# Normalised tokens turned by VectorE in squares of 32 by 32, over a DRAM scratch, instead of by TensorE

## The chip, the cores and the metric

The kernel runs on one core of a Trainium2 chip. The metric is the device time of one execution in microseconds; it is 1164.3 us as a median of three runs (1164.17 to 1164.88).

## What is computed

Input is x, 16 sequences of 1024 tokens with 256 features, in fp32. Two stages, each `x = x + layernorm(f(layernorm(x)))`:

```
g = sigmoid(xn @ Wg.T + bg);  h = scan over the sequence of  h = (1-g)*h + g*xn;  f = h @ Wo.T + bo
router: expert of a token = argmax(xn @ router_w + router_b); rank within the expert < 320 or overflow
f = relu(xn @ w1[e] + b1[e]) @ w2[e] + b2[e]        for a token with a place in its expert (8 of them)
f = relu(xn @ ow1 + ob1) @ ow2 + ob2                for a token that overflowed
```

The kernel sends every token through the overflow path in the loop, and scatters its row (x1, its number and statistics) to its place in a DRAM scratch; the experts then compute the rows that have a place and overwrite their output.

## The kernel before, in words

There are 32 groups of 512 tokens (TG = 4 tiles of 128), two for each sequence; a group is written (i, u), with u its parity. Every fp32 product is made of three fp32r ones (hi*hi, hi*lo, lo*hi), so every operand is split into a hi part by ScalarE and a lo part by VectorE or GpSimd.

The loop is pipelined by groups. In one step TensorE works on the hidden layers (layer1, layer2, eight blocks j of 128 features) of group `now`, on the projection of `nxt` (project) and its transposes (transposes1), and on the transposes (transposes0) and the gate of `far`, which is two groups ahead. `prev` is the group before `now`. The four compute engines run the same steps, each in an order written out by hand; only semaphores tie them.

What belongs to the first normalisation of group far (statistics number 0): VectorE's bn_stats and bn_aggr (read_rows0, moments, in the step before), then two small operations, veps = var + eps and nmean = -mean, still on VectorE; GpSimd makes rstd by pow and nmr = nmean * rstd (deviation, L396), and writes tok = x * rstd + nmr (norm0, L403). TensorE turns tok into psT by eight 128x128 transposes (transposes0, L1330, at j == 3 of the step), ScalarE copies psT to xnT_hi (xn_hi, L644), VectorE takes the rest (xn_lo, L888), and TensorE computes the gate from these at j == 5.

Statistics 1 are those of the attention's output of nxt (ScalarE's norm1, L628, needs them), 2 those of x1 of nxt (deviation2 and norm2, L434 and L443, write tok2 on GpSimd), 3 those of the overflow's output (ScalarE's norm3, L636, for prev).

Order of the step on each engine, before:

- GpSimd (L464): deviation(3, prev), norm0(far), deviation(1, nxt), renumber, norm2(nxt), four indirect stores (dispatch) of now, hst_lo (state_lo) of far.
- VectorE (L1106): low(0, 1), choose, attended and statistics 1 of nxt, residual2(prev), low(2), place(now), low(3), xn_lo(far), residual1(nxt) to x1, statistics 2, low(4, 5), recurrence(far), low(6), read_rows0, low(7), xf_lo(nxt), moments(0), result(now), statistics 3. low(j) is the lo part of hidden block j (L1012).
- ScalarE (L690): blocks 0 and 1, norm3(prev), blocks 2 and 3, xn_hi(far), norm1(nxt), blocks 4 and 5, sigmoid(far), blocks 6 and 7, xf_hi(nxt), state_hi(far).
- SP issues the plain DMAs (L314): the output store of prev, then, after x1 of nxt, the x load three groups ahead.

layer2(now, j) waits for low(j). W1[0], the weights of the first half of the experts, isn't used in the loop.

## Time and profile before

| | before |
|---|---|
| median of three runs | 1164.3 us |
| profiled execution | 1166.17 us, its span 1163.0 us |
| TensorE matmul / weight load busy | 98% / 88% |
| VectorE / ScalarE / GpSimd busy | 85% / 64% / 59% |
| busy share of the 16 DMA engines in the loop | 0.11 |
| mean granted TensorE clock | 0.997 |

The profile is of one execution. Times in it are us from the start of the span; a line such as L1012 is the line of the kernel that issued the instruction. Start-up lasts to about 90 us, the loop with its steady steps to about 950 us, then the last groups and the eight experts follow.

### The profile page before, as it was taken

What the parts mean: (1) busy time and instruction counts of PE and PEld (TensorE: products, weight loads), DVE (VectorE), ACT (ScalarE), POOL (GpSimd) and SP (SyncE); (2) the same over time, 40 slices, a digit from 0 to 9 for tenths busy, and PEclk for the clock granted to TensorE, in tenths of its full rate; (3) what the DMA queues carried; (4) which work ended last, traced back from release to release, by engine and by line L of the source; (5) the groups of instructions that cost most, each with busy time, mean ns of one, the idle gap of its engine ahead of it and who ended that gap; (6) DMA issues with size and microseconds to landing.
All of it is one profiled execution on the core that took longest, in us unless ns stands there. A gap on an engine that the chain in (4) does not pass through costs nothing.

```text
span 1163.0 us, 24424 instructions
## 1 busy us (share of the span) xinstructions
PE 1142.6 (98%) x7549; PEld 1020.4 (88%) x7549; DVE 991.5 (85%) x2741; ACT 742.1 (64%) x1375; POOL 690.1 (59%) x792
## 2 busy tenths in 40 slices
PE   8999999999999999999999999999999999999996
PEld 4788898888988898888888888988898888899996
DVE  6888988888888988989898888888888987688885
ACT  4366666666656666666666666656666666678782
POOL 3556567675656666565657665656666664414444
PEclk9999999999999999999999999999999999999998
DMA  9121110100111111111101101111111100335430
GB/s 262 58 100 56 55 46 35 43 27 30 36 36 36 36 36 36 36 36 36 36 19 35 34 23 33 36 36 36 36 36 36 36 18 20 114 114 191 145 130 34
DMA packets 59428, 65.09 MB, mean 56 GB/s; under 512 B 7835, under 2 KB 55629, under 8 KB 59268
## 3 DMA queue, kind: packets, MB, share of 16 engines
q1 hardware_dynamic: 52228, 59.36, 15.8%
q0 software_dynamic: 7168, 5.34, 1.5%
q8 instruction: 15, 0.25, 0.1%
q14 instruction: 17, 0.14, 0.0%
HBM read 40.19 MB, written 38.76 MB: 68 GB/s over the span
## 4 chain that ended last, share of the span: by engine, by line
PE 90%; DVE 5%; POOL 2%; ACT 1%; issue 1%; DMA 0%; DVEq 0%; POOLq 0%; ACTq 0%
PE psY L1430 12%; PE psY L1433 11%; PE psY L1432 11%; PE psH L1324 11%; PE psH L1325 11%; PE psH L1326 10%; PE psA L1324 5%; PE psA L1325 5%; PE psA L1326 5%; PE psT L1380 3%; PE psT L1337 2%; DVE st L859 1%; PE psT L1393 1%; PE psT L1395 1%; PE psA L1498 1%
## 5 line engine op out<-in xcount | busy, mean ns | idle before, releaser
L621 ACT ACTIVATE hid<-psH,biasT 128x512 f32<-128x512 f32 (+1 forms) x312 | 202.9, 650 | 217.6 <-PE psH L1326 215.2
L1430 PE MATMUL psY<-W_hi,hid_hi 128*128 128x256 f32 x1168 | 336.1, 288 | 0.6 <-DVE hid_lo L1012 0.5
L1433 PE MATMUL psY<-W_hi,hid_lo 128*128 128x256 f32 x1168 | 330.3, 283 | 0.0
L1432 PE MATMUL psY<-W_lo,hid_hi 128*128 128x256 f32 x1168 | 330.2, 283 | 0.0
L399 POOL TENSOR_TENSOR rstd<-veps,mhalf 128x4 f32<-128x4 f32 (+2 forms) x103 | 141.4, 1373 | 163.2 <-DVE nmean L871 163.2
L1012 DVE TENSOR_TENSOR hid_lo<-hid,hid_hi 128x512 fp32r<-128x512 f32 (+1 forms) x308 | 200.6, 663 | 42.5 <-ACT hid_hi L626 35.8
L1324 PE MATMUL psH<-xfT_hi,W_hi 128*128 128x512 f32 (+1 forms) x624 | 235.9, 378 | 0.3 <-ACT hid L621 0.2
L1325 PE MATMUL psH<-xfT_lo,W_hi 128*128 128x512 f32 (+1 forms) x624 | 234.9, 376 | 0.0
L1326 PE MATMUL psH<-xfT_hi,W_lo 128*128 128x512 f32 (+1 forms) x624 | 232.7, 373 | 0.0
L1430 PEld LDWEIGHTS psY<-W_hi,hid_hi 128*128 128x128 f32 x1168 | 222.7, 191 | 9.9 <-DVE hid_lo L1012 1.6
L1432 PEld LDWEIGHTS psY<-W_lo,hid_hi 128*128 128x128 f32 x1168 | 223.0, 191 | 5.9
L1433 PEld LDWEIGHTS psY<-W_hi,hid_lo 128*128 128x128 f32 x1168 | 223.0, 191 | 0.0
L626 ACT ACTIVATE hid_hi<-hid 128x512 fp32r<-128x512 f32 (+1 forms) x308 | 185.2, 601 | 9.8
L421 POOL DMA_INDIRECT xbuf<-x,idx x128 | 144.8, 1131 | 38.4 <-issue 37.8
L437 POOL TENSOR_TENSOR x<-veps,mhalf 128x4 f32<-128x4 f32 x32 | 44.0, 1375 | 173.9 <-DVE nmean L871 173.9
L1326 PEld LDWEIGHTS psH<-xfT_hi,W_lo 128*128 128x128 f32 x624 | 117.2, 188 | 20.9
L1324 PEld LDWEIGHTS psH<-xfT_hi,W_hi 128*128 128x128 f32 x624 | 118.1, 189 | 18.6 <-ACT hid L621 0.8
L1325 PEld LDWEIGHTS psH<-xfT_lo,W_hi 128*128 128x128 f32 x624 | 118.1, 189 | 12.8
L452 POOL TENSOR_SCALAR tok<-x 128x256 f32<-128x256 f32 x116 | 109.0, 951 | 7.7 <-POOL x L440 7.7
L640 ACT ACTIVATE ysb<-ysb,nmr,rstd 128x256 f32<-128x256 f32 x144 | 75.1, 591 | 45.2 <-POOL nmr L401 45.1
L654 ACT ACTIVATE keep<-psA,neg_bg 128x512 f32<-128x512 f32 x64 | 44.1, 689 | 67.9 <-PE psA L1326 62.6
L461 POOL TENSOR_TENSOR hst_lo<-hst,hst_hi 128x512 fp32r<-128x512 f32 x60 | 76.9, 1316 | 3.7 <-ACT hst_hi L662 3.4
(173 smaller groups left out, 2176.8 us busy)
## 6 DMA issues: line engine op xcount, KB each, us to landing
xin<-L_attn_x SPq DMA_DIRECT2D x32, 512.0 KB, 3.4
stage<-L_ffn_w SPq DMA_DIRECT2D x16, 1024.0 KB, 5.2
out<-outt SPq DMA_DIRECT2D x31, 512.0 KB, 2.8
xbuf<-zrow SPq DMA_DIRECT2D x1, 2590.0 KB, 16.5
xin<-xbuf SPq DMA_DIRECT2D x8, 259.0 KB, 4.9
stage<-L_ffn_ow SPq DMA_DIRECT2D x2, 1024.0 KB, 8.5
xbuf<-x,idx POOLq DMA_INDIRECT x128, 2.1
b_b<-L_ffn_b SPq DMA_DIRECT2D x1, 1024.0 KB, 6.5
```

Of the source, the lines that this page charges most:

```text
L399: pool.tensor_tensor(rstd[k][:, t0:n], veps[k][:, t0:n], mhalf[:, t0:n], ALU.pow).then_inc(s_rs[k], 1)
L421: pool.indirect_dma_start(out=xbuf, out_offset=bass.IndirectOffsetOnAxis(idx[v][:, t:t + 1], 0), in_=x1[v][:, t, 0:ROW], in_offset=None, b ...
L452: last = pool.tensor_scalar(tok2[:, t, :], x1[v][:, t, 0:D], x1[v][:, t, D + 1:D + 2], x1[v][:, t, D + 2:D + 3], ALU.mult, ALU.add)
L621: act.activation(hid[j % 2][:, at:n], psH[:, j % 2, at:n], ACT.Relu, bias=bias).then_inc(s_hid, 1)
L626: act.activation(hid_of(j, 0, tail)[:, at:n], hid[j % 2][:, at:n], ACT.Copy).then_inc(s_hid_hi, 1)
L1012: dve.tensor_tensor(hid_of(j, 1, tail)[:, at:n], hid[j % 2][:, at:n], hid_of(j, 0, tail)[:, at:n].bitcast(F32), ALU.subtract).then_inc(s_h ...
L1324: pe.matmul(dst, w_hi, r_hi, start=(k == 0), stop=False)
L1325: pe.matmul(dst, w_hi, r_lo, start=False, stop=False)
L1326: return pe.matmul(dst, w_lo, r_hi, start=False, stop=(k == last_k))
L1430: pe.matmul(dst, hi, w[0][:, j, :], start=(j == 0 and (tail or t % 2 == 0)), stop=False, skip_group_check=True)
L1432: pe.matmul(dst, hi, w[1][:, j, :], start=False, stop=False, skip_group_check=True)
L1433: last = pe.matmul(dst, lo_, w[0][:, j, :], start=False, stop=(j == HC - 1), skip_group_check=True)
```

## The change

Three things are changed.

1. For the groups from (2, 0) on, TensorE's transposes0 in the step is gone. SP waits for tok, stores it (512 KB) to a DRAM scratch `turnbuf` of 512 rows of 256 numbers, waits until it has landed, and issues eight loads. Each fills 32 partitions of one half of `tok_blocks` (in the unused lo part of W1[0]): partition a*32 + x gets, for n = 0 to 15, the 32 numbers `a*32 ..` of the half's columns of row n*32 + x. VectorE then turns the 32x32 squares of both halves into psT, after low(2) and ahead of place.
2. The two small operations at the end of moments go from VectorE to GpSimd, ahead of pow, in all statistics but those of the last expert's tail.
3. On GpSimd norm0(far) comes ahead of deviation(3, prev). On SP the exchange comes ahead of the output store and the x load.

```diff
+        turnbuf = nc.dram_tensor("turnbuf", [GT, D], F32).ap()
+        tok_blocks = late[1][:, 0:TG * D].bitcast(F32).rearrange("p (c n x) -> p c n x", c=DC, x=SQ)
...
+            def exchange_blocks(g):
+
+                i, v = g
+                sp.wait_ge(s_tok, cnt(g, 1, 1))
+                sp.dma_start(turnbuf.rearrange("(t p) d -> p t d", p=P), tok[:]).then_inc(s_turnbuf[v], 16)
+                sp.wait_ge(s_turnbuf[v], landed((i - 2, v)))
+                for a in range(P // SQ):
+                    for c in range(DC):
+                        cols = slice(c * P + a * SQ, c * P + (a + 1) * SQ)
+                        sp.dma_start(tok_blocks[a * SQ:(a + 1) * SQ, c, :, :],
+                                     turnbuf[:, cols].rearrange("(n x) d -> x n d", x=SQ)).then_inc(s_blocks[v], 16)
+
+            def step(i, u, later=True):
+                prev, nxt, turn, far = grp(i, u, -1), grp(i, u, 1), grp(i, u, 2), grp(i, u, 3)
+                if later and live(turn, NG):
+                    exchange_blocks(turn)
                 if live(prev, NG):
                     store(prev)
...
             def deviation(k, g, n, extra=0, t0=0):
 
+                pool.wait_ge(s_ag[k], cnt(g, 1, 1) + extra)
+                pool.sem_inc(s_held, 1)
+                pool.tensor_scalar(veps[k][:, t0:n].unsqueeze(2), mv[k][:, t0:n, 1:2], EPS, None, ALU.add).then_inc(s_ve[k], 1)
+                pool.tensor_scalar(nmean[k][:, t0:n].unsqueeze(2), mv[k][:, t0:n, 0:1], -1.0, None, ALU.mult)
                 pool.wait_ge(s_ve[k], cnt(g, 1, 1) + extra)
...
+                if live(far, NG):
+                    norm0(far)
                 if live(prev, NG):
                     deviation(3, prev, TG, t0=sure(prev))
-                if live(far, NG):
-                    norm0(far)
...
             def moments(k, g, n, base=0, t0=0):
                 dve.wait_ge(s_st[k], cnt(g, 1, 1) + base)
+                dve.wait_ge(s_nm[k], cnt(g, 1, 0) + base)
                 dve.sem_inc(s_held_v, 1)
                 for t in range(t0, n):
                     last = dve.bn_aggr(mv[k][:, t, :], st[k][:, t, :])
                 last.then_inc(s_ag[k], 1)
-                dve.wait_ge(s_nm[k], cnt(g, 1, 0) + base)
-                dve.wait_ge(s_ag[k], cnt(g, 1, 1) + base)
-                dve.tensor_scalar(veps[k][:, t0:n].unsqueeze(2), mv[k][:, t0:n, 1:2], EPS, None, ALU.add)
-                dve.tensor_scalar(nmean[k][:, t0:n].unsqueeze(2), mv[k][:, t0:n, 0:1], -1.0, None, ALU.mult)\
-                    .then_inc(s_ve[k], 1)
...
+            def turn_blocks(g):
+                i, v = g
+                dve.wait_ge(s_blocks[v], landed((i - 2, v), DC * (P // SQ)))
+                for c in range(DC):
+                    dve.transpose(psT[:, c, :], tok_blocks[:, c, :, :]).then_inc(s_T0, 1)
...
                 low(2)
+                if ahead:
+                    turn_blocks(far)
                 if run and up:
                     place(now)
...
-                    if j == 3 and ahead:
-                        transposes0(far)
```

deviation2 gets the same two operations as deviation.

## Rows read from the trace of the kernel before

**Rows 1.** The page: busy time, share of the span and instructions of each engine.
```profile
PE 1142.6 (98%) x7549; PEld 1020.4 (88%) x7549; DVE 991.5 (85%) x2741; ACT 742.1 (64%) x1375; POOL 690.1 (59%) x792
```

**Rows 2.** Stages: window, its us, busy us (count) of each engine, clock, DMA share, GB/s.
```profile
120.00:900.00 780.00, 780.00 (x5159) 699.40 (x5158) 689.33 (x1926) 499.16 (x902) 501.13 (x576) 1.00 0.11 36
...
497.45:528.59 31.14, 31.14 (x207) 27.98 (x207) 27.08 (x76) 19.96 (x36) 21.55 (x25) 1.00 0.11 34
...
1155.00:1160.00 5.00, 0.00 (x0) 0.00 (x0) 0.54 (x1) 0.00 (x0) 2.31 (x3) 0.70 0.18 66
```

**Rows 3.** TensorE in order of time (start, us), and from the waits (total, times, longest).
```profile
508.17 1.04 PE L1337 MATMUL psT<-ident,tok 128*128 128x128 f32 x8
509.04 0.18 PE L1409 MATMUL psA<-oh,upto 128*128 128x32 bf16 x1
...
PEld psT L1337 <- POOL tok L410: 4.5, 14, 0.7
```

**Rows 4.** GpSimd in order of time: start, us, what, [idle before, releaser].
```profile
498.13 2.55 POOL L461 TENSOR_TENSOR hst_lo<-hst,hst_hi 128x512 fp32r<-128x512 f32 x2
501.17 1.42 POOL L399 TENSOR_TENSOR rstd<-veps,mhalf 128x4 f32<-128x4 f32 x1 [0.49 <-DVE nmean L871]
...
503.33 1.01 POOL L399 TENSOR_TENSOR rstd<-veps,mhalf 128x4 f32<-128x4 f32 x1
...
504.86 2.17 POOL L410 TENSOR_SCALAR tok<-xin,rstd,nmr 128x256 f32<-128x256 f32 x4 [0.24 <-POOL nmr L401]
...
516.74 1.41 POOL L437 TENSOR_TENSOR x<-veps,mhalf 128x4 f32<-128x4 f32 x1 [5.79 <-DVE nmean L871]
...
527.67 2.57 POOL L461 TENSOR_TENSOR hst_lo<-hst,hst_hi 128x512 fp32r<-128x512 f32 x2
...
560.47 2.57 POOL L461 TENSOR_TENSOR hst_lo<-hst,hst_hi 128x512 fp32r<-128x512 f32 x2
```

**Rows 5.** ScalarE (one row) and VectorE in order of time.
```profile
503.49 2.08 ACT L640 ACTIVATE ysb<-ysb,nmr,rstd 128x256 f32<-128x256 f32 x4 [0.90 <-POOL nmr L401]
...
508.21 1.23 DVE L942 TENSOR_TENSOR outt<-ysb,x 128x1024 f32<-128x1024 f32 x1
509.36 0.68 DVE L1012 TENSOR_TENSOR hid_lo<-hid,hid_hi 128x512 fp32r<-128x512 f32 x1
509.97 0.18 DVE L994 TENSOR_TENSOR rk<-psA,row 128x32 f32<-128x32 f32 x1
...
515.93 0.38 DVE L866 BATCH_NORM_AGGREGATE mv<-st 128x2 f32<-128x6 f32 x4 [0.16 <-DVE st L859]
...
527.72 2.56 DVE L870 TENSOR_SCALAR veps<-mv 128x4 f32<-128x4 f32 x1
...
548.18 0.38 DVE L866 BATCH_NORM_AGGREGATE mv<-st 128x2 f32<-128x6 f32 x4 [0.16 <-DVE st L859]
```

**Rows 6.** Groups by line and shape: count, busy us, mean ns, idle before.
```profile
L431 POOL TENSOR_SCALAR x<-x 128x4 f32<-128x4 f32 x30 | 8.0, 267 | 2.7
...
L956 DVE TENSOR_TENSOR xfT_lo<-psT,xfT_hi 128x512 fp32r<-128x512 f32 x60 | 38.6, 685 | 13.9 <-ACT xfT_hi L669 13.9
```

**Rows 7.** DMA: KB, landing us; SP's issues; packets, MB, share from 509.61 to 512.41.
```profile
xin<-L_attn_x SPq DMA_DIRECT2D x32, 512.0 KB, 3.4
out<-outt SPq DMA_DIRECT2D x31, 512.0 KB, 2.8
...
514.51 0.38 SPq L272 DMA_DIRECT2D xin<-L_attn_x  x1
...
1009.95 0.48 SPq L343 DMA_DIRECT2D xin<-xbuf  x1
...
q1 hardware_dynamic: 528, 0.52, 52.8%
```

**Rows 8.** DMA packets from 14 to 15 us: number, size, share of 16 engines.
```profile
DMA packets 427, 0.09 MB, mean 89 GB/s; under 512 B 350, under 2 KB 427, under 8 KB 427
...
q1 hardware_dynamic: 427, 0.09, 60.6%
```

More of the change, by code:

```diff
@@ L26 @@
 QUAD = P // TG
+SQ = 32
 EPS = 1e-5
@@ L210, in sandwich_kernel @@
         s_T0 = sem("s_T0")
+        s_blocks = sems("s_blocks")
+        s_turnbuf = sems("s_turnbuf")
         s_xn_hi = sem("s_xn_hi")
@@ L312, in store @@
                     .then_inc(s_st_out[v], 16)
-            def step(i, u):
-                prev, nxt, far = grp(i, u, -1), grp(i, u, 1), grp(i, u, 3)
+            def exchange_blocks(g):
[12 more added lines that the diff above has]
+                    exchange_blocks(turn)
                 if live(prev, NG):
@@ L323, in _ @@
             load((1, 0))
-            step(0, 0)
+            step(0, 0, later=False)
             sp.wait_ge(s_ow_hi, 4)
@@ L329, in _ @@
             load_w2((0, 0))
-            step(0, 1)
+            step(0, 1, later=False)
             with sp.Fori(1, NG // 2 - 2) as i:
@@ L435, in deviation2 @@
                 i, v = g
+                pool.wait_ge(s_ag[2], cnt(g, 1, 1))
+                pool.sem_inc(s_held, 1)
+                pool.tensor_scalar(veps[2][:].unsqueeze(2), mv[2][:, :, 1:2], EPS, None, ALU.add).then_inc(s_ve[2], 1)
+                pool.tensor_scalar(nmean[2][:].unsqueeze(2), mv[2][:, :, 0:1], -1.0, None, ALU.mult)
                 pool.wait_ge(s_ve[2], cnt(g, 1, 1))
```

## The prediction

> **What bounds the kernel now.** I read the page first, then the table by stage, then one step of the loop engine by engine. The page gives TensorE 98% busy and VectorE 85% [rows 1]. That is an average; the table by stage says more: from 120 to 900 us TensorE is busy 780.00 of 780 us, and one step of the loop takes 31.14 us, all of it matrix work, at a granted clock of 1.00 [rows 2]. So in the steady loop nothing but TensorE sets the time, and an edit that leaves every other engine in time is worth what it takes off TensorE. Reading one step in order of time shows how much room the others have, and that is the question here, because the change lengthens one of their paths. That path is a ring, once around per step:
>
> 1. VectorE's last bn_aggr on x1 ends (515.93 + 0.38 = 516.31) [rows 5].
> 2. GpSimd ends those statistics, writes tok2, issues four scatters and does hst_lo, until 527.67 + 2.57 = 530.24: 13.93 us [rows 4, 5]. In the step of the other parity the same stretch runs from 548.56 to 563.04: 14.48. I take 14.2.
> 3. GpSimd ends statistics 3, then 0, and writes tok (one step earlier 500.68, by the same period, to 504.86 + 2.17 = 507.03: 6.35 us) [rows 4].
> 4. TensorE turns tok (0.9 us), and ScalarE copies it, then normalises att.
> 5. VectorE does place, low(3), xn_lo, the residual to x1 and its statistics, without a gap from 509.97 to 516.31: 6.34 us [rows 5].
>
> These make 14.2 + 6.35 + 0.9 + 6.34 = 27.8 us against a step of 31.14: about 3.3 us of room. That is little: TensorE's weight loads for these transposes waited for GpSimd's tok 14 times already [rows 3].
>
> **The change part by part.** The trace's own time is 1166.2 us (span 1163.0); the median of the runs is 1164.3, 1.9 below. The sum is made against 1166.2. The scratch serves 28 groups, from (2, 0) to (15, 1), one in each step of TensorE's loop; the first two groups and the two after them keep TensorE's transposes, the experts have none.
>
> *Taken away.* Eight transposes per step: the first starts at 508.17, the next work of TensorE at 509.04 [rows 3], so 0.87 us. If all else is in time: 28 x 0.87 = 24.4 us, a step of 30.27, and 1142.
>
> *Statistics.* VectorE loses two small operations per moments, and with them a stall: at 527.72 veps took 2.56 us, beside GpSimd's hst_lo of 2.57 that had begun at 527.67 [rows 5, 4]. GpSimd gains two operations on 128x4. The nearest row is its 128x4 tensor_scalar, 267 ns [rows 6], so 0.54 us for each statistics, 2.2 us per step. In stretch 2 it starts 0.43 us sooner (at 516.31 instead of 516.74), so that net +0.1 to 0.2: 14.4. The order on GpSimd is turned: norm0(far) ahead of deviation(3). Stretch 3 loses statistics 3 thereby: pow of 0 to the end of tok takes 507.03 - 503.33 = 3.70 [rows 4], plus 0.54 is 4.24 us. Behind norm0 now stands deviation(3), for which ScalarE's norm3, VectorE's residual2 and what is queued behind it wait (a rival below). With the experts, statistics moved to GpSimd cost nothing: TensorE's work there covers them. Uncovered, 8 x 0.54 = 4 us.
>
> The Trainium skill (SBUF — State Buffer, section SBUF: two separate sides) says that VectorE's operations in a 2-port mode and GpSimd's hold a shared port pair as an exclusive lock. The row of veps beside hst_lo agrees. Were this the bound, moving the operations would gain; the step is TensorE's, so by this rule alone the sum stays.
>
> *The exchange.* It goes in place of TensorE's 0.9 us between tok and psT.
> (a) SP waits for tok and stores 512 KB: the output store, of the same size and packets, lands 2.8 us after its issue [rows 7]; with 0.1 for the wait, 2.9.
> (b) SP waits for that store to land, and then issues eight loads of 64 KB, in 128-byte pieces: 4096 packets, 256 on each of 16 engines. Nothing in the trace has this form. The store's 512 packets of 1 KB moved in 52.8% of 16 x 2.8 us, so 46 ns each, 1.5 us per engine; the x loads (same packets) land after 3.4 us [rows 7], so about 1.85 us of a load's time is fixed. Cheapest: packets so cheap that SP's issue bounds. At 0.38 to 0.48 us an issue [rows 7] the eighth goes out 3.0 us after the first; with its own packets and 1.85 that is 5.2 us. Dearest: a 128-byte packet takes as long as one of 1 KB: 256 x 0.046 = 11.8, and 1.85: 13.6 us. Between them lies the one microsecond of the trace with mostly small packets (14 to 15 us: 350 of 427 under 512 bytes): busy 60.6% of 16 us, 22.7 ns per packet; by elapsed time 37 ns [rows 8]. I take 23 ns, as the nearest row: 256 x 0.023 = 5.9, and 1.85: **7.75 us**. By elapsed time it would be 11.3.
>
> On SP the exchange stands ahead of store(prev) and load(far). The output store is needed only two steps later. The x load waits for x1, which comes later in the step. Neither is late.
>
> *The sum of the ring.* 14.4 + 4.24 + 2.9 + 7.75 + 1.38 + 6.34 = **37.0 us**. The wait for the blocks stands ahead of place, low(3), xn_lo and residual1 on VectorE, which wait with it; TensorE's layer2(3) waits for low(3), and scatters, hst_lo and the next norm0 come after. So the ring closes, and since 37.0 is more than TensorE's 30.27, the step becomes 37.0 us: +5.9 against 31.14, times 28 is 164 us. 1166.2 + 164 = **1330 us**.
>
> Bounds: stretch 2 at 13.9 + 0.2 and the exchange at 5.2 give 34.2 us a step, 1252 us; the loads at 11.3 give 40.6, 1430; at 13.6, 42.9, 1495. TensorE would wait 4 us at a time. It does so only at the end of this trace: 5 us without work, granted clock 0.70 [rows 2], so on its way to 1.2 GHz. Its stretch from low(3) to hst_hi has some 3 us of room against GpSimd's, so a short fall costs little; a long one up to 3 us a step, which is why the high end isn't lower.
>
> **Rivals.**
> *Cheap packets* (the same ring): 34.2 to 35.8 us a step, 1252 to 1296. For it: a packet of 1 KB takes 46 ns, and if time went by bytes alone, 128 bytes would take 6.
> *Dear packets*, 30 ns and more: over 39.3 us a step, over 1394. For it: the elapsed time of the small packets above.
> *The order on GpSimd decides, not the transfer.* With an exchange that costs nothing extra the path would go tok, deviation(3) (2.2 us: 501.17 to 503.33), ScalarE's norm3 (2.08), residual2 (1.23), low(2) (0.68), turn [rows 4, 5]: 14.4 + 4.24 + 2.2 + 2.1 + 1.2 + 0.7 + 1.38 + 6.34 = 32.6 us, so +1.4 per step, 1207 us. It decides if store and loads together take less than 6.2 us.
> *The other side: hidden, and TensorE stays the bound.* The step is 30.27 us, 1142 us. It needs a ring of at most 30.27, so that 6.7 us of my 37.0 are not there: store and loads in 3.9 us together, where the two fixed parts alone, 1.3 and 1.85, and the issues take 6, and statistics 3 off the path. For it: VectorE loses its stalls, and GpSimd's operations could be shorter beside an idle VectorE. Against it: both would have to give several us.
> *It doesn't do what it says*: VectorE's turn into PSUM has no fast form or the blocks come out in parts; that adds 1.4 us a step or more, inside the range.
>
> **How the numbers follow.** Ring with 6.5 to 10 us for the loads (1296 to 1394): 0.47, forecast 1330. Cheap packets: 0.24. Dear packets: 0.14. Order on GpSimd (1207): 0.08. Hidden (1142): 0.05. Within 0.2% (a ring of 31, by chance): 0.02. The range 1245 to 1430 leaves out the last three and about a third of the dear ones. Faster 0.05, same 0.02, slower 0.93; 0.2% is about what a measurement of this kernel can tell from no change.
>
> **What would show it.** Right: the steady step at 34 to 40 us; VectorE idle before the transposes, released by a DMA; TensorE idle before the layer-2 matmuls, released by hid_lo; TensorE's busy share near 85%; the chain of waits going through GpSimd and DMA. GpSimd's idle time before deviation2 and norm0 small. Wrong: a step near 30.3 with TensorE full (the packets cost far less, or the ring has slack I did not see); VectorE idle before residual2 instead (the order decides); blocks that land 5 or 12 us after the store did (the price of a packet).

## The result, and the profile after

| | before | after |
|---|---|---|
| median | 1164.46 us (1164.17 to 1164.88) | 1309.74 us (1308.39 to 1311.0) |
| ratio, 95% interval | | 1.1247 (1.1228 to 1.1267) |
| span of the profiled execution | 1163.0 us | 1306.8 us |
| mean granted TensorE clock | 0.997 | 0.968 |

The change makes the kernel 12.5% slower. The forecast was 1330 us, from 1245 to 1430.

The page of after: busy time, share of the span and instructions of each engine, then two DMA issues (KB each, median us from issue to landing); then the stage that answers to [rows 2].

```profile
PE 1179.0 (90%) x7325; PEld 1018.8 (78%) x7325; DVE 977.2 (75%) x2527; ACT 737.6 (56%) x1375; POOL 751.3 (57%) x1062
...
turnbuf<-tok SPq DMA_DIRECT2D x28, 512.0 KB, 2.8
W_lo<-turnbuf SPq DMA_DIRECT2D x224, 64.0 KB, 2.3
...
120.00:900.00 780.00, 704.09 (x4317) 606.35 (x4316) 590.00 (x1537) 428.81 (x781) 481.76 (x680) 0.96 0.23 60
```

TensorE, which had no gap in this stage before [rows 2], now has 76 us of gaps (780.00 less 704.09), and needs longer for its work: 224 matmuls fewer over the whole run, but 36.4 us more of busy time than in [rows 1]. With the 24.4 us of the transposes that are gone, its work takes some 61 us longer. By the granted clock, 0.968 on average instead of 0.997, some 38 of them are a slower clock (an estimate from the span). The rest comes with the waits: the profile models where a matmul ends (here 0.28 us after its start, while the next ones start 0.12 apart), and before a wait it counts the last one as busy up to that end.

The issues of SP in one step show the period (start, us, what):

```profile
498.30 0.36 SPq L324 DMA_DIRECT2D turnbuf<-tok  x1
501.08 4.04 SPq L329 DMA_DIRECT2D W_lo<-turnbuf  x8
...
534.52 0.36 SPq L324 DMA_DIRECT2D turnbuf<-tok  x1
```

From store to store it is 534.52 - 498.30 = **36.22 us**, where it was 31.14 [rows 2]. This is one of the longer steps. From one group's place to the next (TensorE's first matmul of it, psA<-oh,upto, once for each group) the mean of 22 steps is 35.96 us, from 35.4 to 36.7; before it was 31.17. The 4.8 us times 28 steps are 134 us. The spans differ by 143.8 us: 136.5 of it between the first and the last group's place, 1.1 ahead of it and 6.2 behind, with the experts (170.5 us instead of 164.3). So nearly all of the loss is one of the loop, about the same in each step. The chain of waits by engine, before and after, says what the time consists of, and then the chain itself in order of time, from tok to the turn:

```profile
PE 90%; DVE 5%; POOL 2%; ACT 1%; issue 1%; DMA 0%; DVEq 0%; POOLq 0%; ACTq 0%
...
POOL 27%; PE 22%; issue 15%; DVE 14%; DMA 11%; SPq 7%; ACT 3%; POOLq 1%; DVEq 0%; ACTq 0%
...
498.30 2.77 DMA turnbuf<-tok
501.08 0.32 SPq L329
501.40 0.05 issue
501.45 0.48 SPq L329
...
504.63 2.38 DMA W_lo<-turnbuf
507.02 0.06 DVE psT L923
```

The chain goes through GpSimd, the DMAs, SP and VectorE; TensorE, with 90% of this chain on the page of before, has 22% of it here. Between 501.08 and 504.63 it is SP that is followed: it hands out the eight loads, the second after 0.37 us and each further one after 0.53, and only the last one's landing is waited for. VectorE and GpSimd in order of time, with the idle time before and its releaser, close the ring (these answer to [rows 4, 5]):

```profile
507.02 1.32 DVE L923 STREAM_TRANSPOSE psT<-W_lo 128x512 f32<-128x512 f32 x2 [2.68 <-DMA W_lo<-turnbuf]
...
514.06 0.38 DVE L895 BATCH_NORM_AGGREGATE mv<-st 128x2 f32<-128x6 f32 x4 [0.18 <-DVE st L887]
...
514.63 0.46 POOL L462 TENSOR_SCALAR veps<-mv 128x4 f32<-128x4 f32 x1 [10.19 <-DVE mv L895]
515.17 0.53 POOL L463 TENSOR_SCALAR nmean<-mv 128x4 f32<-128x4 f32 x1
515.67 1.03 POOL L465 TENSOR_TENSOR x<-veps,mhalf 128x4 f32<-128x4 f32 x1
516.78 0.91 POOL L468 TENSOR_TENSOR x<-nmean,x 128x4 f32<-128x4 f32 x1
517.94 3.73 POOL L480 TENSOR_SCALAR tok<-x 128x256 f32<-128x256 f32 x4 [0.24 <-POOL x L468]
...
527.23 2.54 POOL L489 TENSOR_TENSOR hst_lo<-hst,hst_hi 128x512 fp32r<-128x512 f32 x2
529.86 0.56 POOL L420 TENSOR_SCALAR veps<-mv 128x4 f32<-128x4 f32 x1
...
532.32 2.18 POOL L434 TENSOR_SCALAR tok<-xin,rstd,nmr 128x256 f32<-128x256 f32 x4 [0.30 <-POOL nmr L425]
```

GpSimd has no gap from 514.63 to 534.50 but for short ones, then tok is stored, and the ring starts again. From 498.30 to 514.44 SP, the DMAs and VectorE have the ring; GpSimd does statistics 3 and 1 meanwhile, and then idles for 10.19 us until 514.63. TensorE's side of it, and its clock behind the gap (window, its us, busy us of its matmuls, granted clock, DMA share, GB/s):

```profile
510.16 0.58 PE L1462 MATMUL psY<-W_hi,hid_hi 128*128 128x256 f32 x1 [2.67 <-DVE hid_lo L1042]
...
507.60:511.00 3.40, 0.84 (x4) 0.86 0.05 18
511.00:515.00 4.00, 4.00 (x18) 0.69 0.27 90
```

It waits 2.67 us for low(3), which stands on VectorE behind the turn, and then works 4 us at a granted clock of 0.69, so part of this time at 1.2 GHz.

Against the steps of the prediction, each as it has it, measured in the step shown (36.22 us; the mean is 35.96):

| part of the ring | predicted | measured |
|---|---|---|
| x1's bn_aggr end to hst_lo end | 14.4 | 15.33 (514.44 to 529.77) |
| first normalisation, to the end of tok | 4.24 | 4.73 (to 534.50) |
| store | 2.9 | 2.78 |
| eight loads | 7.75 (5.2 to 13.6) | 5.94 (501.08 to 507.02) |
| turn | 1.38 | 1.23 (to 508.25, where place begins) |
| place to bn_aggr end | 6.34 | 6.19 (508.25 to 514.44) |
| sum | 37.0 | 36.2 |

### The profile page after: what moved, and what is told of

Its sections match the earlier page's. It is cut to its first block, busy times and chain, and to the rows that moved or that the text cites. A ratio compares the mean times of both kernels' runs of the same rounds, so it can differ in the third digit from the quotient of the medians.

```text
span 1306.8 us, 24281 instructions
## 1 busy us (share of the span) xinstructions
PE 1179.0 (90%) x7325; PEld 1018.8 (78%) x7325; DVE 977.2 (75%) x2527; ACT 737.6 (56%) x1375; POOL 751.3 (57%) x1062
## 4 chain that ended last, share of the span: by engine, by line
POOL 27%; PE 22%; issue 15%; DVE 14%; DMA 11%; SPq 7%; ACT 3%; POOLq 1%; DVEq 0%; ACTq 0%
SPq L329 7%; DMA turnbuf<-tok 6%; POOL hst_lo L489 5%; DMA W_lo<-turnbuf 5%; POOL xbuf L445 5%; POOL tok L434 4%; PE psY L1462 3%; POOL rstd L423 3%; DVE st L887 3%; PE psY L1465 3%; PE psY L1464 3%; PE psH L1356 2%; PE psH L1357 2%; PE psH L1358 2%; POOL tok L480 2%
## 5 line engine op out<-in xcount | busy, mean ns | idle before, releaser
L1462 PE MATMUL psY<-W_hi,hid_hi 128*128 128x256 f32 x1168 | 346.9, 297 | 77.6 <-DVE hid_lo L1042 77.6
L1465 PE MATMUL psY<-W_hi,hid_lo 128*128 128x256 f32 x1168 | 338.0, 289 | 0.0
L1464 PE MATMUL psY<-W_lo,hid_hi 128*128 128x256 f32 x1168 | 337.4, 289 | 0.0
L1464 PEld LDWEIGHTS psY<-W_lo,hid_hi 128*128 128x128 f32 x1168 | 230.0, 197 | 3.7
L1465 PEld LDWEIGHTS psY<-W_hi,hid_lo 128*128 128x128 f32 x1168 | 230.6, 197 | 0.0
L462 POOL TENSOR_SCALAR veps<-mv 128x4 f32<-128x4 f32 x32 | 14.2, 442 | 309.0 <-DVE mv L895 308.9
L445 POOL DMA_INDIRECT xbuf<-x,idx x128 | 138.2, 1080 | 38.2 <-issue 38.2
L423 POOL TENSOR_TENSOR rstd<-veps,mhalf 128x4 f32<-128x4 f32 (+2 forms) x103 | 106.9, 1038 | 0.0
L923 DVE STREAM_TRANSPOSE psT<-W_lo 128x512 f32<-128x512 f32 x56 | 36.9, 705 | 75.0 <-DMA W_lo<-turnbuf 75.0
L420 POOL TENSOR_SCALAR veps<-mv 128x4 f32<-128x4 f32 (+2 forms) x103 | 31.0, 301 | 93.8 <-DVE mv L895 88.5
```

The source lines that it names most:

```text
L423: pool.tensor_tensor(rstd[k][:, t0:n], veps[k][:, t0:n], mhalf[:, t0:n], ALU.pow).then_inc(s_rs[k], 1)
L445: pool.indirect_dma_start(out=xbuf, out_offset=bass.IndirectOffsetOnAxis(idx[v][:, t:t + 1], 0), in_=x1[v][:, t, 0:ROW], in_offset=None, b ...
L1462: pe.matmul(dst, hi, w[0][:, j, :], start=(j == 0 and (tail or t % 2 == 0)), stop=False, skip_group_check=True)
L1464: pe.matmul(dst, hi, w[1][:, j, :], start=False, stop=False, skip_group_check=True)
L1465: last = pe.matmul(dst, lo_, w[0][:, j, :], start=False, stop=(j == HC - 1), skip_group_check=True)
```

## Experiments

All are compared with runs of the kernel before on the same chip, whose medians lay between 1164.4 and 1165.0 us. Diffs are against after unless it is said that they are against before.

**1. No exchange.** VectorE turns tok itself, as soon as GpSimd has written it; the store and the loads are gone.

```diff
-                if later and live(turn, NG):
-                    exchange_blocks(turn)
...
-                dve.wait_ge(s_blocks[v], landed((i - 2, v), DC * (P // SQ)))
+                dve.wait_ge(s_tok, cnt(g, 1, 1))
```

> The changed kernel without its exchange: no store, no loads; VectorE turns the squares of tok itself as soon as tok is written, so the gate is computed from tokens in a wrong arrangement (this part of the computation is changed; its amount is not). Ring theory with the transfer as the price: the step loses the 8.75 us from the end of tok to the landed blocks, and what ends last then is GpSimd's order (norm0, statistics 3, norm3 on ScalarE, residual2, low(2), turn: 6.0 us by the rows of the changed kernel), so 36.2 - 8.75 + 6.0 = 33.5 us a step, about 1232 us. Rival 1, nothing else but TensorE bounds once the transfer is gone: 30.3 us, 1142 us. Rival 2, the transfer was not the price but VectorE's extra work or the slower clock: close to 1300 us.

Measured: 1228.61 us, ratio 1.0544 (1.0526 to 1.0561). That is what the ring on GpSimd's order gives, and not what a full TensorE gives. The waits of ScalarE and VectorE from 120 to 900 us (us in total, times, longest):

```profile
ACT ysb L666 <- POOL nmr L423: 132.4, 24, 5.5
...
DVE outt L970 <- ACT ysb L666: 47.9, 23, 2.1
```

In every step norm3 waits 5.5 us for the end of statistics 3, which now stand behind tok, and residual2 waits 2.1 us for norm3. The step is 33.14 us here (mean of 22), near the 33.5 expected. So of the 145 us, 81 go with the transfer; the other 64 are still there without it.

**2. Four loads instead of eight.** The same 4096 packets, in loads of 128 KB.

```diff
-                    for c in range(DC):
-                        cols = slice(c * P + a * SQ, c * P + (a + 1) * SQ)
-                        sp.dma_start(tok_blocks[a * SQ:(a + 1) * SQ, c, :, :],
...
+                    sp.dma_start(tok_blocks[a * SQ:(a + 1) * SQ],
+                                 turnbuf.rearrange("(n x) (c f) -> x c n f", x=SQ, c=DC)[:, :, :, a * SQ:(a + 1) * SQ])\
```

> The same exchange with four loads of 128 KB instead of eight of 64 KB; number and size of packets are the same. If SP's issue sets the time of the loads (eighth issued 3.55 us after the first, 0.53 us each, landed 2.4 us later), four issues fewer take 2.1 us from the ring: 34.1 us a step, about 1250 us. If the packets set it (256 to an engine, by elapsed time 23 ns each), nothing changes: 1310 us.

Measured: 1289.67 us, ratio 1.1064 (1.1045 to 1.1082): 20 us less, between the two. SP's issues and the landing of a load:

```profile
531.58 2.91 SPq L327 DMA_DIRECT2D W_lo<-turnbuf  x4
...
W_lo<-turnbuf SPq DMA_DIRECT2D x112, 128.0 KB, 3.1
```

The four issues take 2.91 us together where eight took 4.04: an issue is not of constant length; for these loads it grows with the packets, from about 0.49 us for 512 to about 0.67 for 1024 (a median of single issues). And the landing takes 3.1 instead of 2.3 us. So neither theory holds alone. What the loads cost is mostly SP's issuing, and half of what merging saves there is lost in the landing of the last.

**3. Statistics 3 ahead of the first normalisation again** (GpSimd's order of before, everything else as after).

```diff
-                if live(far, NG):
-                    norm0(far)
                 if live(prev, NG):
                     deviation(3, prev, TG, t0=sure(prev))
+                if live(far, NG):
+                    norm0(far)
```

> The changed kernel with GpSimd's old order: statistics 3 of prev ahead of norm0(far). Ring theory: statistics 3 (1.9 us: two small operations, pow, product) come into the ring again, 38.1 us a step, about 1362 us. If the path over norm3 and residual2 set the step, it would be faster than the changed kernel: below 1300 us.

Measured: 1427.86 us, ratio 1.2256 (1.2220 to 1.2292), much more than expected: +118 us against after, 4.2 a step. GpSimd in that kernel:

```profile
499.79 0.24 POOL L420 TENSOR_SCALAR veps<-mv 128x4 f32<-128x4 f32 x1 [1.70 <-DVE mv L895]
...
504.55 3.65 POOL L434 TENSOR_SCALAR tok<-xin,rstd,nmr 128x256 f32<-128x256 f32 x4 [0.30 <-POOL nmr L425]
```

The two things that the expectation left out stand in these rows: GpSimd waits 1.70 us for statistics 3, and tok then lies where it takes 3.65 us instead of 2.18. With the 1.9 us of statistics 3 they make 5.1 us in this step; tok is as long as this in most steps and not in all, and the steps, 38.5 or some 41 us long, are 4.5 us longer than after's on average. So given an exchange, the new order is a gain, and a large one.

**4. The store twice**, one after the other.

```diff
-                sp.wait_ge(s_turnbuf[v], landed((i - 2, v)))
+                sp.wait_ge(s_turnbuf[v], (i - 2) * 32 + 16)
+                sp.dma_start(turnbuf.rearrange("(t p) d -> p t d", p=P), tok[:]).then_inc(s_turnbuf[v], 16)
+                sp.wait_ge(s_turnbuf[v], (i - 2) * 32 + 32)
```

> The changed kernel with the scratch written twice, the second store after the first has landed, the loads after the second. It adds a pure delay of one store, 2.8 us, to the exchange and no work to a compute engine. Ring theory: all of it shows, 39.0 us a step, +78 us, about 1388 us. If the loads were hidden behind something else, by less than a delay of 2.8 us, less than that; if the exchange doesn't matter: 1310 us.

Measured: 1391.31 us, ratio 1.1942 (1.1917 to 1.1968): 81.6 us for 28 x 2.8 = 78. What is added between tok and the turn is paid in full: the ring is closed and nothing in it is hidden.

**5. The exchange a step early.** GpSimd normalises the group three ahead, right after norm2; the scatters go behind statistics 3 of the next step; SP exchanges after the x load. On VectorE moments(0) goes ahead of xf_lo. The other edits only follow from these.

```diff
-                if live(far, NG):
-                    norm0(far)
...
+                dispatch(prev, range(TG))
...
+                if live(grp(i, u, 3), NG):
+                    norm0(grp(i, u, 3))
                 if live(far, NG):
                     state_lo(far)
```

> A version that keeps the exchange and takes it off the ring: GpSimd normalises group +3 right after norm2 (so a step's second half ahead), SP exchanges it after its x load, and the scatters of prev come after statistics 3 of the next step, in GpSimd's idle time; VectorE ends statistics 0 ahead of xf_lo. Ring theory, by the rows of the changed kernel: from bn_aggr on x1 to tok2 7.2 us, to the end of statistics 0 0.7, norm0 4.6, exchange 8.75, turn 1.3, place to bn_aggr 6.2: 28.8 us, less than TensorE's 30.3. So TensorE is the bound again: 30.3 us a step, about 1142 us, faster than the kernel before by the eight transposes. Rival: the small packets, or VectorE's extra 1.4 us, or GpSimd's statistics cost of their own: 1165 us or more even so.

Measured: 1181.83 us, ratio 1.0151 (1.0137 to 1.0164): 128 us of the 145 come back, but it isn't faster than before. In order of time, the turn, and the only wait of TensorE's matmuls that the profile lists in the loop, one in each step, with its row; then TensorE's stage and the part where the experts begin:

```profile
514.60 1.31 DVE L924 STREAM_TRANSPOSE psT<-W_lo 128x512 f32<-128x512 f32 x2
...
PE psA L1357 <- POOL hst_lo L489: 11.8, 25, 0.7
...
600.07 0.36 PE L1357 MATMUL psA<-WoT_hi,hst_hi 128*128 128x256 f32 x1 [0.45 <-POOL hst_lo L489]
...
120.00:900.00 780.00, 767.63 (x4951) 673.41 (x4950) 679.60 (x1776) 498.72 (x901) 539.49 (x775) 1.00 0.27 69
...
1020.00:1060.00 40.00, 36.13 (x262) 34.06 (x263) 30.00 (x66) 27.83 (x58) 7.71 (x12) 1.00 0.41 129
```

The turn waits for nothing: store and loads are hidden altogether. The 12 us of gaps in the loop are waits for hst_lo, which now stands behind tok. Outside it TensorE has some 12 us more of gaps than before: where the experts begin, from 1020 to 1060 us, it is busy 36.13 of 40 us. The gaps sum to 44.7 us, against 20.4 before. And TensorE's busy time is only 7.4 us below that of [rows 1], not the 24 us that the eight transposes of 28 steps were taken to be worth. So the 40 us that are missing to 1142 are 24 of gaps (44.7 less 20.4) and 17 of busy time.

The busy time is waiting too, as the order of TensorE's matmuls shows. The step is 31.21 us (mean of 22), where it was 31.17: nothing of the 0.87 us is won. TensorE's projection of nxt, released by hst_lo, starts 0.83 to 0.88 us after the matmul before it, where in before it starts after 0.23 in every step; and the transposes of tok2 start about 0.2 us late in the same way. Together that is nearly the 0.87 us, and the profile lists half of it as gaps and counts the rest as busy, up to the modelled end of the last matmul. So the transfer is hidden, but a ring over GpSimd's order, which now has tok ahead of hst_lo, holds the step where TensorE had held it. The 16.9 us by which the spans differ lie outside the steady steps: 9.0 behind the last group's place (173.3 us instead of 164.3), the rest ahead of it, in the start and the first and last steps.

**6. Only the scatters moved** behind statistics 3 of the next step.

```diff
                 if live(prev, NG):
                     deviation(3, prev, TG, t0=sure(prev))
+                dispatch(prev, range(TG))
...
-                if live(now, NG):
+                if last:
                     dispatch(now, range(TG))
```

> The changed kernel with one thing moved: the four scatters of a group stand after statistics 3 of the next step, not between norm2 and hst_lo. Ring theory: 5.6 us of GpSimd's stretch go, but hst_lo then waits for ScalarE's hst_hi (524.6 in the changed kernel, hst_lo could start at 521.7), so 3.1 us of it show: 33.1 us a step, about 1221 us. Rival, the time goes by the transfer alone: 1310 us.

Measured: 1252.35 us, ratio 1.0753 (1.0736 to 1.0769): 57 us less than after, 2.0 a step, where four scatters (5.4 us from 521.84 to 527.23) leave the ring. The rest is taken by a new wait of GpSimd in each step (group by line: busy, mean ns, idle before and its releaser):

```profile
L489 POOL TENSOR_TENSOR hst_lo<-hst,hst_hi 128x512 fp32r<-128x512 f32 x46 | 58.7, 1297 | 57.1 <-ACT hst_hi L690 57.1
```

hst_lo is now reached 2.5 us before ScalarE's hst_hi is ready (57.1 us in 23 steps), and it is issued in order, so the normalisation behind it waits too.

**7. The small operations back on VectorE** (veps and nmean of all statistics), the rest as after.

```diff
-                pool.tensor_scalar(veps[k][:, t0:n].unsqueeze(2), mv[k][:, t0:n, 1:2], EPS, None, ALU.add).then_inc(s_ve[k], 1)
-                pool.tensor_scalar(nmean[k][:, t0:n].unsqueeze(2), mv[k][:, t0:n, 0:1], -1.0, None, ALU.mult)
...
+                dve.tensor_scalar(veps[k][:, t0:n].unsqueeze(2), mv[k][:, t0:n, 1:2], EPS, None, ALU.add)
+                dve.tensor_scalar(nmean[k][:, t0:n].unsqueeze(2), mv[k][:, t0:n, 0:1], -1.0, None, ALU.mult)\
```

> The changed kernel with veps and nmean back on VectorE in all statistics, exchange and order kept. Ring theory: statistics 2 lose 0.46 + 0.53 us on GpSimd and start 0.35 us later, norm0 loses 0.55: 1.2 us less in the ring, 35.0 us a step, about 1276 us. Rival: on VectorE they wait for GpSimd's hst_lo (2.56 us once in the rows of before) and that shows: 1310 us or more.

Measured: 1281.77 us, ratio 1.1015 (1.0999 to 1.1032): 28 us less than after, 1.0 a step. In the loop the statistics on GpSimd are a loss, near the size of their operations: 20 of the 28 us are won there, 0.7 a step. The rest is won outside it: with the statistics on VectorE again, the time behind the last group's place is 164.0 us, as before, and not 170.5. So the moved statistics cost 6 us in the experts.

**8. Statistics and order, without the exchange**: after with TensorE's transposes.

```diff
-                if later and live(turn, NG):
-                    exchange_blocks(turn)
...
-                if ahead:
-                    turn_blocks(far)
...
+                    if j == 3 and ahead:
+                        transposes0(far)
```

> The kernel before with the second and third part of the change alone: statistics on GpSimd, norm0 ahead of statistics 3; tok goes to psT by TensorE's transposes as before, and there is no exchange. Ring theory: the ring is about 28 us, TensorE's 31.1 us stay the bound, 1164 us. Rival: the moved statistics or the later norm3 cost something by themselves: above 1170 us.

Measured: 1214.69 us, ratio 1.0433 (1.0419 to 1.0447). A miss, and the most telling one: the part of the change that has nothing to do with a transfer costs 50 us by itself. No wait of TensorE for tok is in this trace; as in experiment 1, norm3 waits for statistics 3 (134.6 us in 24 steps) and TensorE for tok2 and hst_lo (16.5 and 9.0 us), and the chain of waits runs over GpSimd's order. The step is 32.65 us. The next two runs take the 50 us apart.

**9. The order alone.** Against before:

```diff
+                if live(far, NG):
+                    norm0(far)
                 if live(prev, NG):
                     deviation(3, prev, TG, t0=sure(prev))
-                if live(far, NG):
-                    norm0(far)
```

> The kernel before with one edit: on GpSimd the first normalisation of group far stands ahead of statistics 3 of prev. TensorE's transposes and VectorE's small operations stay. The ring then goes stretch 2 (14.2 us), pow of statistics 0 to the end of tok (3.70), statistics 3 (2.2), norm3 (2.08), residual2 (1.23), low(2) (0.68), place to bn_aggr (6.34): 30.4 us, under TensorE's 31.14, so 1164 us or a few more. If the order by itself carries the 50 us that order and statistics cost together, it is near 1214 us.

Measured: 1175.22 us, ratio 1.0091 (1.0074 to 1.0108). The order alone costs 10 us; in its trace no wait of TensorE for tok is left, while norm3 waits for statistics 3 for 100.0 us in 25 steps. The step is 31.52 us for 31.17, and that is the 10 us. Most of it is lost at TensorE's projection, which waits for GpSimd's hst_lo (first hst_lo and projection here, then the projection of before):

```profile
565.18 2.57 POOL L461 TENSOR_TENSOR hst_lo<-hst,hst_hi 128x512 fp32r<-128x512 f32 x2
567.90 0.36 PE L1324 MATMUL psA<-WoT_hi,hst_hi 128*128 128x256 f32 x1
...
563.31 0.28 PE L1324 MATMUL psA<-WoT_hi,hst_hi 128*128 128x256 f32 x1
```

Here the projection starts 0.15 us after hst_lo's end in every step, and 0.50 to 0.53 us after the matmul before it instead of 0.23: some 0.28 us of the 0.35 a step. Before, it started 1.9 us after hst_lo's end in one parity and 0.27 in the other (563.04 [rows 4] to 563.31). So this hand-over too had room in one step and next to none in the other.

**10. The statistics alone.** Against before: the two operations on GpSimd, in deviation and deviation2, as in the change.

```diff
+                pool.tensor_scalar(veps[k][:, t0:n].unsqueeze(2), mv[k][:, t0:n, 1:2], EPS, None, ALU.add).then_inc(s_ve[k], 1)
+                pool.tensor_scalar(nmean[k][:, t0:n].unsqueeze(2), mv[k][:, t0:n, 0:1], -1.0, None, ALU.mult)
```

> The kernel before with one edit: the two small operations of all statistics on GpSimd. Order, transposes and the rest as before. The ring is 14.4 + 2.74 (statistics 3) + 4.24 (first normalisation) + 0.9 + 6.34 = 28.6 us, still under 31.14: the loop costs nothing, and only the experts lose about 6 us, as TensorE's waits there in the runs with these statistics show: 1170 us. If the statistics carry the 50 us by themselves, it is near 1214 us.

Measured: 1213.80 us, ratio 1.0432 (1.0410 to 1.0455): 49 us. Some 7 of it lie ahead of the first and behind the last group's place, about what was expected for the experts; the rest is in the loop. TensorE and GpSimd in a step of that kernel, the longest of tok's four operations and the one of VectorE beside it, and TensorE's waits from 120 to 900 us:

```profile
528.62 1.09 PE L1365 MATMUL psT<-ident,tok 128*128 128x128 f32 x8 [2.38 <-POOL tok L432]
...
520.29 0.47 POOL L418 TENSOR_SCALAR veps<-mv 128x4 f32<-128x4 f32 x1 [1.74 <-DVE mv L893]
520.84 0.57 POOL L419 TENSOR_SCALAR nmean<-mv 128x4 f32<-128x4 f32 x1
...
522.79 0.23 POOL L418 TENSOR_SCALAR veps<-mv 128x4 f32<-128x4 f32 x1
523.11 0.23 POOL L419 TENSOR_SCALAR nmean<-mv 128x4 f32<-128x4 f32 x1
...
524.86 3.71 POOL L432 TENSOR_SCALAR tok<-xin,rstd,nmr 128x256 f32<-128x256 f32 x4 [0.24 <-POOL nmr L423]
...
525.94 2.09 POOL L432 TENSOR_SCALAR tok<-xin,rstd,nmr 128x256 f32<-128x256 f32 x1
525.89 1.19 DVE L970 TENSOR_TENSOR outt<-ysb,x 128x1024 f32<-128x1024 f32 x1
...
PE psT L1365 <- POOL tok L432: 28.9, 12, 2.5
```

In every second step TensorE stands 2.4 us before its transposes. The path to them is: TensorE's last psY of a group, VectorE's ysb and statistics 3, GpSimd's ends of statistics 3 and 0, tok, transposes. GpSimd puts 0.47 + 0.57 + 0.23 + 0.23 = 1.5 us more into it, and tok itself, pushed to another place beside VectorE's work, takes 3.71 us instead of 2.18. The two make 3.0 us. From VectorE's last bn_aggr of statistics 3 to the end of tok it is 8.5 us here (520.08 to 528.57), where before has 5.7 in the step without room (533.51 to 539.26) and 6.3 in the other, so 2.7 us or 2.2 more, against a wait of 2.4 and a little room. So the dear thing was a path that my ring did not contain. It is not the path of experiment 8, though that run loses the same 50 us: there TensorE does not wait for tok.

**11. A pure delay in before.** SP stores tok twice to a scratch that nobody reads; TensorE waits for the second store before its transposes. Against before:

```diff
+                sp.dma_start(turnbuf.rearrange("(t p) d -> p t d", p=P), tok[:]).then_inc(s_turnbuf0[v], 16)
+                sp.wait_ge(s_turnbuf0[v], landed((i - 2, v)))
+                sp.dma_start(turnbuf.rearrange("(t p) d -> p t d", p=P), tok[:]).then_inc(s_turnbuf1[v], 16)
...
                     if j == 3 and ahead:
+                        pe.wait_ge(s_turnbuf1[far[1]], landed((far[0] - 2, far[1])))
                         transposes0(far)
```

> The kernel before, with a pure delay between tok and TensorE's transposes: SP stores tok to a scratch twice, one after the other, and TensorE waits for the second. Each store takes 2.9 us, so the ring of before is 5.8 us longer. With the 3.3 us of room that the prediction read from the trace, the step is 33.6 us, +2.5 against 31.14, times 28: 1234 us. With no room at all +5.8 a step: 1327 us; with all of it hidden: 1164 us.

Measured: 1342.67 us, ratio 1.1521 (1.1498 to 1.1543): +178 us, 6.3 a step for 5.8 of delay, beyond even the end "no room". TensorE, and its clock behind the wait:

```profile
520.52 1.94 PE L1352 MATMUL psT<-ident,tok 128*128 128x128 f32 x8 [4.52 <-DMA turnbuf<-tok]
...
520.50:525.00 4.50, 4.48 (x25) 4.44 (x26) 2.25 (x10) 3.10 (x6) 0.00 (x0) 0.50 0.33 117
```

TensorE waits 4.52 us, then works 4.5 us at a granted clock of 0.50, which is 1.2 GHz, so half of that time, 2.2 us, is lost on top. Of the 5.8 us some 1.3 were hidden in this step, and 2.1 in the step of the other parity, where TensorE waits 3.7 us: that is the room. The mean of the two waits, 4.1 us, and the 2.2 for the clock are the 6.3 us a step. The trace of before has less still, and I had not looked there: one step in the two has tok end at 507.03 and the transposes start at 508.17, 1.14 us later [rows 3, 4], in the other step the two rows are

```profile
539.31 1.09 PE L1337 MATMUL psT<-ident,tok 128*128 128x128 f32 x8
...
537.08 2.18 POOL L410 TENSOR_SCALAR tok<-xin,rstd,nmr 128x256 f32<-128x256 f32 x4 [0.29 <-POOL nmr L401]
```

with 0.05 us between them (539.26 to 539.31).

**12. The early exchange with the small operations on VectorE and hst_lo ahead of it.** Against the kernel of experiment 5, besides the edit of experiment 7:

```diff
-                if live(grp(i, u, 3), NG):
-                    norm0(grp(i, u, 3))
                 if live(far, NG):
                     state_lo(far)
+                if live(grp(i, u, 3), NG):
+                    norm0(grp(i, u, 3))
```

> The exchange hidden as in the run with the early normalisation, with two more edits: the small operations of the statistics go back to VectorE, and GpSimd does hst_lo ahead of the early normalisation, so that TensorE no longer waits for it (0.5 us a step there). If these two are what kept that run at 1182 us, the step comes near TensorE's 30.3 and the experts lose nothing: 1142 us, and in any case under 1164. If the 0.9 us of removed transposes are not all there to be had, 1155 to 1170 us; if statistics 3, now 4 us later on GpSimd, hold up residual2 and low(2), over 1182 us.

Measured: 1199.88 us, ratio 1.0302 (1.0285 to 1.0319), 18 us more than experiment 5. GpSimd shows why (the exchange is late again, and VectorE's turn waits 1.4 us a step for it, 33.8 us in 24 steps):

```profile
507.45 4.37 POOL L472 TENSOR_SCALAR tok<-x 128x256 f32<-128x256 f32 x4 [0.29 <-POOL x L460]
514.26 2.55 POOL L481 TENSOR_TENSOR hst_lo<-hst,hst_hi 128x512 fp32r<-128x512 f32 x2 [2.44 <-ACT hst_hi L683]
516.77 1.01 POOL L419 TENSOR_TENSOR rstd<-veps,mhalf 128x4 f32<-128x4 f32 x1
```

Between tok2 and hst_lo GpSimd stands idle for 2.44 us, and that is the slot which the early normalisation had filled. The two edits are not told apart by this run. No version here beats before.

## Why the prediction was right, and where it was not

*What bounds the kernel after.* Right. The ring was named with its six parts, and 36.2 us were measured for 37.0 in one step, 36.0 on average. Experiments 4 (a store more is paid in full) and 1 (without the transfer the next path in line decides) show that it is closed and that the transfer is in it.

*The price of the loads.* The forecast took 23 ns a packet and 7.75 us; measured are 5.94. The step that failed is that packets bound. In the window of the loads 4456 packets took 67.2% of 16 engines over 5.94 us; 232 of them are the output store's, of 1 KB and 46 ns each, and the 4096 of 128 bytes took 12.7 ns each. With that, the engines have room, and SP's issuing decides: the eighth load goes out 3.55 us after the first and lands 2.38 us later, 5.93 together, which is the cheap end's form. The cheap end's number, 5.2, was too low since it took an issue at 0.38 to 0.48 us from loads with few packets [rows 7]; these take 0.49 and a gap. So the rival "cheap packets" had the mechanism. That the sum still came to 37.0 is partly luck: the loads were 1.8 us too dear, and the stretches on GpSimd 1.4 too cheap. So the sum of the loop, 164 us, was 27 too high against the 136.5 measured, and some of it was made up outside the loop, where nothing had been put down and 7 us were lost.

*GpSimd's statistics.* The two operations were put at 0.27 us each; those of x1 took 0.46 and 0.53, beside VectorE's recurrence, and nmr in that place 0.91. Stretch 2 took 15.33 for 14.4. Experiment 7 gives 0.7 us a step for them in all, and 6 us more in the experts. There the prediction had them cost nothing, covered by TensorE's work, or 4 us uncovered; they were not covered.

The Trainium skill (SBUF — State Buffer, section SBUF: two separate sides) has VectorE's and GpSimd's port pair as an exclusive lock, and from it I took only what moving VectorE's stalled operations could gain. In experiment 10 VectorE no longer has these operations, and GpSimd's tok took 3.71 us instead of 2.18. The trace fits such a lock: three of tok's four operations take 0.55 us and one takes 2.09, the one that starts 0.05 us after VectorE's outt. But the lock has a cost on either side, and I had counted one.

*The order and what comes with it.* That statistics and order cost nothing beyond their places in the ring was tacit in the sum, and it was wrong for a kernel without the exchange: the statistics alone cost 49 us (experiment 10), the order alone 10 (9), both 50 (8). Within the sum of the loop it did no harm, because the parts don't add: the paths run side by side, and the longest sets the step. Statistics, order and exchange together cost 145; taking the transfer out gives back 81, taking the statistics out 28, and taking the order out costs 118 more. The rival "the order on GpSimd decides" was worked out as 1207 us for a transfer that costs nothing, and experiment 1, which is that case, gave 1229: a right mechanism, 0.5 us a step too cheap (33.14 for 32.6), and 7 us outside the loop.

*The room of before.* "About 3.3 us of room" is the plain error. It went by one ring, the one that the change lengthens, and left out that TensorE's transposes stand in TensorE's own order: what comes late there delays all that TensorE has behind them, and it has no gap to catch up. Experiment 11 shows 1.3 us of room in one step and 2.1 in the other, the rows of before 1.14 in one step and 0.05 in the next. The 14 waits of the weight loads [rows 3] were the sign of it: one in every second step. The forecast escaped it only because the change takes TensorE out of this very path.

*The clock.* It was foreseen that TensorE would wait about 4 us at a time and lose clock; it waits 2.67 here, and loses some of it. Its work in the step from 498.30 to 534.52 takes 32.66 us, 1.5 more than the 31.14 of [rows 2] with eight transposes fewer; that is filled into its gaps. The ring doesn't pass through it, and GpSimd has no gap while it works slower, so nothing of it shows in the step; in experiment 11, where TensorE is in the ring, the clock costs 2.2 us a step.

*The other side.* "Hidden, 1142 us" did not happen, and experiment 5, in which the exchange is hidden, shows that this is no question of the transfer alone: it gives 1182. Taking the transposes away is worth its 24.4 us only where the other rings leave it, and none is left there: the step stays at 31.2 us, held by hst_lo. So the path over hst_lo stands as close to TensorE's 31.1 us as the one over tok, and it would have had to be shortened as well.

## What to carry to other kernels

Before a step is put into a loop, list every closed path through it, those that go through the full engine's own order among them, and read the room of each in both parities of the loop, at the row where one engine hands over to the other: the smallest counts. A chain of a store and loads over DRAM costs its two landings and one issue per load (here 2.8 and 2.4 us, and 3.55 for the issues), so it pays only where it is started that much before its data are needed. An operation moved to a second engine has to be priced where it will stand, since the work beside it may nearly double its time, and what is queued behind it moves too.

## What the runs showed of the hardware

- A load of 128-byte packets keeps an engine busy 12.7 ns per packet, against 46 ns for one of 1 KB [rows 7]: over a quarter of the time for an eighth of the bytes.
- The time that SP takes to issue a load of 128-byte packets grows with their number: about 0.49 us for 512, about 0.67 for 1024. It is not the number alone: the store has 512 packets too, of 1 KB, and takes 0.36.
- VectorE's transposes of 32x32 squares of fp32 from SBUF into PSUM take 705 ns for 128x512 (mean of 56 in after), about as long as its other passes of this shape over psT, 685 ns [rows 6].
- GpSimd's tok, the same four operations of 128x256, takes from 2.18 us to 3.7, by where it stands beside VectorE's work; tok2, of the same shape, was seen at 3.08, 3.73, 4.37 and 4.58, and in experiment 11 at 2.18.
- After 2.67 us of waiting TensorE worked 4 us at a granted clock of 0.69; after 4.52 us (experiment 11), 4.5 us at 0.50.
